# Gathering the query rows of destinations by indirect DMA in the fourth edge stage of a graph network kernel

## What is computed

```python
q = (tfn_features @ Wq).reshape(n, H, DQK)            # 8 heads of 16
x_dst = tfn_features[edge_dst]
wk = mlp2(edge_features, k_w1, k_b1, k_w2, k_b2)      # [E, 128]
wv = mlp2(edge_features, v_w1, v_b1, v_w2, v_b2)
k = tensor_product(x_dst, edge_sh, wk, Cqk)           # w * sum_s sh[:, s] * (x @ C[:, s, :]), s = 0..8
v = tensor_product(x_dst, edge_sh, wv, Cv)
attn = jnp.einsum('ehd,ehd->eh', q[edge_src], k)
# softmax over the edges of each node (segment max, exp, segment sum), then
upd = jax.ops.segment_sum(v * alpha[..., None], edge_src, num_segments=n) @ W_out
out = tfn_features @ W_self + upd                     # then batch norm, scale, shift
```

## Time and profile before

| | us |
|---|---|
| median of three runs | 3517.68 (3505.01 to 3533.71) |
| profiled execution | 3510.65 |
| its span, first to last instruction | 3508.9 |
| PE busy | 2551.3 (73%) |
| DVE busy | 2280.8 (65%) |
| POOL busy | 1789.0 (51%) |
| ACT busy | 1062.1 (30%) |

### The profile page before, as it was taken

One profiled execution on the slowest core, in us unless ns is written; L12 is line 12 of the kernel. 1 busy time (PEld: TensorE's weight loads), 2 busy tenths in 40 slices (PEclk: granted clock), 3 DMA queues, 4 the chain that ended last, 5 costly groups with the idle time before them and its releaser, 6 DMA issues. The chain is left out here.

```text
span 3508.9 us, 58176 instructions
## 1 busy us (share of the span) xinstructions
PE 2551.3 (73%) x14132; PEld 2166.8 (62%) x14132; DVE 2280.8 (65%) x5044; ACT 1062.1 (30%) x2723; POOL 1789.0 (51%) x1813
## 2 busy tenths in 40 slices
PE   3778777514554444357777765999999999999986
PEld 2778776413443333245555544888888888888872
DVE  3555555337887887855556542677777777777775
ACT  1111111134554564111111101344444344443441
POOL 2777776066666663157777723444444344443400
PEclk7776777556555666589999967999999999999985
DMA  2443443265554552035445517988888888888830
GB/s 64 93 87 84 87 87 64 46 161 131 132 123 125 132 124 72 2 110 157 153 153 161 158 63 177 203 204 197 197 201 199 200 198 190 193 200 198 195 92 9
DMA packets 433884, 475.50 MB, mean 136 GB/s; under 512 B 200837, under 2 KB 304648, under 8 KB 433712
## 3 DMA queue, kind: packets, MB, share of 16 engines
q1 hardware_dynamic: 358832, 295.60, 35.9%
q0 software_dynamic: 59904, 123.64, 15.2%
q10 hardware_dynamic: 14976, 54.53, 4.5%
HBM read 408.18 MB, written 65.34 MB: 135 GB/s over the span
## 5 line engine op out<-in xcount | busy, mean ns | idle before, releaser
L1960 PE MATMUL psum<-ckv,z 128*128 128x256 f32 x4160 | 969.7, 384 | 0.0
L1960 PEld LDWEIGHTS psum<-ckv,z 128*128 128x128 f32 x4160 | 767.9, 191 | 98.5
L1823 POOL DMA_INDIRECT ga<-XX,src_i x416 | 398.1, 957 | 449.7 <-PE psum L1941 307.0
L985 POOL DMA_INDIRECT ga<-T,src_i x416 | 431.4, 1037 | 302.3 <-issue 112.5
L275 POOL DMA_INDIRECT ga<-T,src_i x416 | 401.3, 965 | 151.7 <-issue 124.4
L275 POOL DMA_INDIRECT ga<-TA,src_i x416 | 412.4, 991 | 126.7 <-issue 126.7
L2009 DVE TENSOR_TENSOR z<-psum,shb 128x2560 f32<-128x2560 f32 x104 | 293.7, 2824 | 125.8 <-PE psum L1941 78.5
L455 PE MATMUL psum<-wre,re 128*128 128x68 f32 x832 | 213.4, 349 | 142.1 <-DVE oneT L331 82.6
L1816 POOL TENSOR_TENSOR acc<-acc,wkv 128x512 f32<-128x512 f32 x104 | 114.3, 1099 | 332.7 <-DMA wkv<-WKV 316.4
L455 PEld LDWEIGHTS psum<-wre,re 128*128 128x128 f32 x832 | 173.4, 258 | 162.9 <-issue 153.9
L2050 DVE TENSOR_TENSOR acc<-acc,psum 128x256 f32 x416 | 175.4, 422 | 120.2 <-PE psum L1932 90.9
(11 more groups left out here) (349 smaller groups left out, 4862.8 us busy)
## 6 DMA issues: line engine op xcount, KB each, us to landing
shb<-in_ea SPq DMA_DIRECT2D x104, 640.0 KB
WKV<-wkvo ACTq DMA_DIRECT2D x104, 512.0 KB
shb<-in_ea SPq DMA_DIRECT2D x104, 512.0 KB
wkv<-WKV SPq DMA_DIRECT2D x104, 512.0 KB
dl<-DL SPq DMA_DIRECT2D x312, 128.0 KB, 3.5
acc<-QW SPq DMA_DIRECT2D x416, 64.0 KB
win<-TB SPq DMA_DIRECT2D x416, 32.0 KB
ga<-T,src_i POOLq DMA_INDIRECT x832
```

Of the source, the lines that this page charges most:

```text
L985: pool.indirect_dma_start(ga[:, ring(g) + t, :], None, T1, bass.IndirectOffsetOnAxis(ap=src_i[:, g * GT + t:g * GT + t + 1], axis=0)).then ...
L1823: pool.indirect_dma_start(ga[:, (g % GR) * GT + t, :], None, XX, bass.IndirectOffsetOnAxis(ap=src_i[:, g * GT + t:g * GT + t + 1], axis=0) ...
L1960: last = pe.matmul(kv_of(k)[:, t, :], z[:, k % 2, j, t * 128:(t + 1) * 128], ckv[:, j, :], start=(j == 0), stop=(j == NZ - 1))
```

## The change

The query path by windows goes. Instead POOL gathers the query row of each edge's destination by indirect DMA, four a group, right behind the gather of features of the next group (`queries`), into a ring of four groups. DVE multiplies them with the weights at the head of `keys_and_values`. The loads of windows and places, ACT's three operations, PE's four matmuls and POOL's multiply are left out. The load of the weights loses its wait for POOL's multiply; it stays at two steps behind the harmonics. QW needs no padding rows any more, and the destinations of padding edges (-1) are raised to 0 by one DVE operation while the tables are made.

```diff
@@ tables of the fourth stage
-        QW = dram("QW", [NW, F])
+        QW = dram("QW", [N, F])
...
-                sp.dma_start(QW[N:NW, :], zero[:, 0:F]).then_inc(n3_o, 16)
...
                 ln_relu_steps(c, n3_var, n3_std, 1, XC=XC)
+                c.link(dve.tensor_scalar(dst_i[:], dst_i[:], 0, None, ALU.max))
                 dve.wait_ge(n3_p, 5)
...
+        QR = 4
+        e3_gq = [sem(f"e3_gq{k}") for k in range(UG)]
...
-        oneT = acc[:, 2, 0:2 * GT * W].rearrange("p (a e) -> p a e", a=2)
-        qs = acc[:, 2, 2 * GT * W:4 * GT * W].rearrange("p (a e) -> p a e", a=2)
-        win = acc[:, 2, 4 * GT * W:4 * GT * W + WR * GT * F].rearrange("p (t f) -> p t f", f=F)
+        qg = acc[:, 2, 0:QR * GT * F].rearrange("p (t f) -> p t f", f=F)
...
             def _(pool):
-                def weighted_query(g):
-                    slot = g % 2
-                    pool.wait_ge(e3_q, g + 1)
-                    pool.wait_ge(e3_n[slot], (g // 2 + 1) * 16)
-                    q = qs[:, slot, :].rearrange("p (t f) -> p t f", t=GT)
-                    pool.tensor_tensor(q, q, wkv[:, slot, :, 0:F], ALU.mult).then_inc(e3_wq, 1)
+                def queries(g):
+                    if g >= QR:
+                        pool.wait_ge(e3_ev, (g - QR + 1) * 2)
+                    for t in range(GT):
+                        pool.indirect_dma_start(qg[:, (g % QR) * GT + t, :], None, QW, bass.IndirectOffsetOnAxis(
+                            ap=dst_i[:, g * GT + t:g * GT + t + 1], axis=0)).then_inc(e3_gq[g % UG], 16)
...
-                    if g > GR:
-                        weighted_query(g - GR - 1)
-                for g in range(groups - GR - 1, groups):
-                    weighted_query(g)
+                    if g:
+                        queries(g - 1)
+                queries(groups - 1)
@@ SP
                 def weights_load(i, k):
                     g = i * UG + k
-                    wait(sp, e3_wq, g - 1)
-                    sp.sem_inc(e3_sp, 1)
                     wait(sp, e3_ev, (g - 1) * 2)
...
-                        wait(sp, e3_oT, g - 1)
-                        sp.sem_inc(e3_sp, 1)
-                        sp.dma_start(dl[:, k % 2, :], DL[:, cols].partition_broadcast(128)).then_inc(e3_dl[k % 2], 16)
...
-                        window_loads(win, sp, i, k, QW, F, e3_w, e3_Q, e3_sp, ring=WR)
@@ ACT: queries(i, k) and places(i, k) and their calls
-                    act.activation(qs[:, k % 2, :], bank[1][:], ACT.Copy).then_inc(e3_q, 1)
...
-                    act.activation(o, dl[:, k % 2, :], ACT.Abs, bias=iota_p[:, 0:1], scale=-1.0).then_inc(e3_ta, 1)
-                    act.wait_ge(e3_ta, g + 1)
-                    act.activation(o, o, ACT.Relu, bias=ones_c[:, 0:1], scale=-1.0).then_inc(e3_oT, 1)
@@ PE: queries(i, k) and its call
-                    for t in range(GT):
-                        last = pe.matmul(bank[1][:, t * 128:(t + 1) * 128], oneT[:, k % 2, t * 128:(t + 1) * 128],
-                                         win[:, (k % WR) * GT + t, :], start=True, stop=True)
@@ DVE
                 def keys_and_values(i, k):
                     g = i * UG + k
                     s, kk = k // KG, k % KG
+                    dve.wait_ge(e3_gq[k], i * 64 + 64)
+                    dve.wait_ge(e3_n[k % 2], i * (UG // 2 * 16) + (k // 2 + 1) * 16)
+                    q = qg[:, k % QR * GT:(k % QR + 1) * GT, :]
+                    dve.tensor_tensor(q, q, wkv[:, k % 2, :, 0:F], ALU.mult).then_inc(e3_wq, 1)
                     dve.wait_ge(e3_V, g + 1)
                     dve.wait_ge(e3_wq, g + 1)
                     wait(dve, e3_s, g)
                     three = lambda v: v.rearrange("p (t f) -> p t f", t=GT)
-                    dve.tensor_tensor(three(kt), kv_of(k)[:, :, 0:F], three(qs[:, k % 2, :]), ALU.mult).then_inc(e3_ev, 1)
-                    dve.wait_ge(e3_n[k % 2], i * (UG // 2 * 16) + (k // 2 + 1) * 16)
+                    dve.tensor_tensor(three(kt), kv_of(k)[:, :, 0:F], q, ALU.mult).then_inc(e3_ev, 1)
```

More of the change, by code:

```diff
@@ L1704, in _ @@
                 sp.wait_ge(n3_qc, len(rounds(NJ, 4)))
-                sp.dma_start(QW[0:N, :].rearrange("(j p) f -> p j f", p=PN), tab[:]).then_inc(n3_o, 16)
-                sp.wait_ge(n3_o, 4 * 16)
+                sp.dma_start(QW.rearrange("(j p) f -> p j f", p=PN), tab[:]).then_inc(n3_o, 16)
+                sp.wait_ge(n3_o, 3 * 16)
                 sp.wait_ge(n3_l, NL3 * 16)
@@ L1758, in build @@
         e3_g = [sem(f"e3_g{k}") for k in range(UG)]
-        WR = 2
-        e3_w = [sem(f"e3_w{k}") for k in range(WR)]
+        QR = 4
+        e3_gq = [sem(f"e3_gq{k}") for k in range(UG)]
         e3_e = [sem(f"e3_e{k}") for k in range(2)]
         e3_n = [sem(f"e3_n{k}") for k in range(2)]
[L1763 to L1766, removed]
+        (e3_one, e3_oa, e3_X, e3_z, e3_wq, e3_V, e3_ev, e3_s, e3_S, e3_acc, e3_M, e3_Mx, e3_i, e3_pad, e3_sp) = [
+            sem("e3_" + x) for x in
+            ("one", "oa", "X", "z", "wq", "V", "ev", "s", "S", "acc", "M", "Mx", "i", "pad", "sp")]
         S3 = softmax_sems("b3", bank[7])
@@ L1773, in build @@
         one = tmp("one3", [128, OR * GT, 128])
-        dl = tmp("dl3", [128, 2, GT * W], BF16)
         wkv = tmp("wkv", [128, 2, GT, 2 * F])
@@ L1900, in body @@
                     p1, p2 = soft_1(i, k), soft_2(i, k)
-                    if lag(i, k, 1):
-                        queries(*lag(i, k, 1))
                     if p1:
                         softmax_act_1(act, S3, p1[0] * 2 + p1[1], 8)
-                    if lag(i, k, 0):
-                        places(i, k)
                     if p2:
@@ L1942, in transposes @@
                     last.then_inc(e3_X, 1)
[L1944 to L1948, removed]
-                    for t in range(GT):
-                        last = pe.matmul(bank[1][:, t * 128:(t + 1) * 128], oneT[:, k % 2, t * 128:(t + 1) * 128],
-                                         win[:, (k % WR) * GT + t, :], start=True, stop=True)
-                    last.then_inc(e3_Q, 1)
                 def products(i, k, t):
@@ L1972, in body @@
                         transposes(i, k)
-                    if kv:
-                        queries(*kv)
                     if p1:
```

## The result

The changed kernel takes 3530.0 us (median; 3527.18 to 3534.63) against 3517.68 (3505.01 to 3533.71). The ratio is 1.004, with a 95% interval of 1.0021 to 1.0059: 0.4% slower, within the 1% of "no difference that can be told" and 6 us from the forecast. On another chip the same kernel was 8.8% slower than the kernel before (experiment 8). The profiled execution's span is 3525.4 us, 16.5 above that of before.

What follows compares the result with a forecast made beforehand. PE was taken as the bound by a small margin, DVE right behind. Terms 2 - 9 + 17 = +10 us gave 3520.7 on the profiled execution and 3527.7 for the median; the forecast between them was 3524 us, range 3488 to 3564.

Steps and rivals of the forecast that it cites:

- What bounds the kernel: Fourth edge stage: PE bound by a small margin, DVE right behind; PE's second sums wait for DVE's first addition.
- The price of the multiply: DVE, ahead of keys_and_values: the new multiply costs d = 0.80 us a step, bounds 0.69 and 1.10.
- dearer, 1.10 or more: Rival: DVE's new multiply costs 1.10 us or more a step, +29 us more, 3553 us; chance 0.20.
- The iteration: Eight steps of the stage's loop: 95.5 us against 95.3 before, DVE eating PE's 7.2; +2 us over 12 iterations.
- after k = 7 it starts 5.1: Loop's turn: DVE's z starts 5.1 us into PE's step k = 0, which then takes 14.8 us.
- The clock: TensorE's clock falls behind PE's standstill at k = 0: 2.3 us in 85% of twelve turns, less 6.8, +17 us.
- The first steps: First eight steps, without sums, PE alone: 5 us from the queries and 4 from POOL's multiply, -9 us in all.
- Queues and gathers: SP, POOL and DMA queues: the weights' load and the gathers stay hidden; eight gathers take 10.0 of some 11.9 us.
- The sum: Whole kernel: 2 - 9 + 17 = +10 us on the profiled execution's 3510.65 us, giving 3520.7 us.
- PE keeps its gain: Rival: the 94 us of queries' work taken off PE come through whole, 3420 us; chance 0.10.

Runs made afterwards that it cites:

- experiment 8: Another chip, kernel before 3868.68 us: changed kernel 4204.18 us (1.0879); with a second DVE multiply 4211.23 us; late multiply, unlooped DVE and extra PE matmuls 4172.99 us.
- Experiment 1: Changed kernel with four unused matmuls put back on PE in each step, where the queries' matmuls stood: 3553.81 us, ratio 1.0126 to the kernel before.
- experiment 2: Changed kernel with DVE's new multiply done one step earlier, behind the addition of the first sums: 3491.39 us, ratio 0.9955 to the kernel before.
- experiment 3: Changed kernel with sixteen unused matmuls on PE at k = 0, ahead of its second sums: 3510.35 us, ratio 1.0002 to the kernel before.
- experiment 4: Changed kernel without query gathers from the ninth group on, old rows multiplied again: 3529.45 us, ratio 1.0054 to the kernel before.
- experiments 6 and 7: 6: DVE's stage program unlooped: before 3464.37, changed 3444.75, changed with late multiply 3406.08 us. 7: the last plus four unused PE matmuls per step: 3461.88 us.

## Why the prediction came out

**What bounds the kernel: right.** PE the bound by a small margin, DVE right behind it, and the second sums the place where they meet. Experiment 1 shows it from one side (0.9 us more on PE change nothing in k = 2, 3, 4), experiment 2 from the other.

**The price of the multiply: right.** d = 0.80 was taken; the rows give 0.77 in a plain step and 0.88 at the turn (2422.84 - 2421.96), and L1976 itself is 0.686, L2033 was 0.687. The rival "dearer, 1.10 or more" fell with it. The Trainium skill's rule (SBUF — State Buffer, Who interferes with whom) that a GpSimd instruction reading SBUF blocks DVE's with two SBUF inputs holds for POOL's tensor_tensor (before, every L598 of over 430 ns overlaps L1816; without it the median went from 835 to 429 ns) but not for gathers: 57 of the 104 multiplies overlap one, and the longest took 704 ns.

**The iteration: right in its steps, short at the turn.** By step, in us:

| k | before | predicted | after |
|---|---|---|---|
| 1, 5 | 11.30 | 10.39 | 10.40 |
| 2, 6 | 11.87 | 11.94 | 12.11, 12.01 |
| 3, 7 | 11.87 | 12.33 | 12.36 |
| 4 | 11.30 | 11.39 | 11.38 |
| 0, without the clock's fall | 13.93 | 14.8 | 15.6 |
| sum | 95.3 | 95.5 | 96.6 |

The 13.93 is one turn (the eleven of before take 14.15 on average without the falls); the 15.6 is the mean of eleven (18.1) less 2.45; experiment 3, with the clock held, shows 15.44 to 15.83. Of the 1.1 us, k = 2 and 6 have 0.24 and the turn 0.8. In k = 2 DVE allowed the second sums 0.05 us later than worked out, and PE's part behind them took 3.18 instead of 3.06: where PE has stood, its first pair of second sums takes 0.49 us instead of 0.39. At the turn the step "after k = 7 it starts 5.1" is the one that was off: z came 5.6 to 6.3 us behind PE, because the issue pause was 3.6 to 4.3 us and not the 3.33 of the earlier trace rows (3.0 to 3.4 in all turns before), and DVE waited 0.65 us for the exponents ahead of L1994, where it was 0.30 before (L2033). Why the pause grew is not shown. Without the clock this term is +12 over ten iterations, where it was +2 over twelve.

**The clock: right in kind, a little short in size.** Taken were 2.3 us in 85% of twelve turns. It fell in all eleven turns of the loop, behind standstills of 4.7 to 5.5 us, and cost 2.2 to 2.8 us each time, 26.9 in all, less 6.8: +20 instead of +17. The twelfth "turn" is the entry into the loop, where PE stood only 1.06 us in the changed kernel; the prediction had counted it, and the 4.57 us of before there were POOL's doing. Experiment 3 confirms the clock as a cost of its own: with it held, k = 0 is 2.4 us shorter. The price does not follow the standstill alone: in experiment 1 PE stood 3.8 to 4.2 us at each turn, and the part behind took 4.5 to 4.6 us in five turns and 5.7 in six. The Trainium skill (TensorE: Matmul & The Clock Gate, Part 1: The HAM clock gate) has the array fall to half rate after idle stretches; the windows agree (PEclk 0.99, then 0.50, behind a stretch with PE at 0.00).

**The first steps: near.** -9 predicted for the first eight with POOL's lead; the first sixteen gave -12.3 (80.5 + 99.93 to 75.31 + 92.85 us), 2.3 of it the clock's. The first eight alone gave -5.2; 4.4 more lie in the entry into the loop, where DVE no longer waits for POOL's multiply.

**Queues and gathers: right.** Hidden, by experiment 4.

**The sum.** Predicted -9 + 2 + 17 = +10. Measured in the spans: -10 in the first sixteen steps without the clock, +12 in the ten iterations without it, +20 for the clock, together +22.3 in the stage; -5.8 around it, +16.5; in the medians +12.3. The iteration's term was too small by 10 us and the clock's by 3. The 6 us ahead of the stage, which nobody predicted, hid a part, and they are scatter. That the forecast was closer than its terms is luck.

**The rival "PE keeps its gain"** is false for this kernel and true for a neighbour: with the multiply late and the turn gone, the same change is worth 58 us and PE is the bound again (experiments 6 and 7), for the wait that gave its gain away is nearly gone.

## What to carry to other kernels

Work taken off the busiest engine is worth only the slack of the engine that it waits for: before moving an operation onto that one, write down for each step of the unrolled body when it releases the other, and count the operation only where it lies ahead of that release. Then place it behind the release; here the order alone was worth 0.85%, more than the change. A loop's turn is paid by the engine that has no slack left there, and the other's standstill is paid twice when its clock falls.

## What the runs showed of the hardware

- A turn of DVE's loop costs 3.0 to 3.4 us of "issue" before z in the kernel before and 3.6 to 4.3 in the changed one; written out, there is none, and the kernel before alone gains 1.4% (48 us, against 3512.05 on the same chip).
- TensorE's granted clock went to 0.50 at all eleven turns where PE had stood 4.7 to 5.5 us. Before, it fell behind standstills of 2.09, 2.95 and 4.57 us and held behind nine of 2.25 to 2.89. A fall cost 1.6 to 2.8 us in the matmuls behind it, and sixteen idle matmuls in the gap prevented it.
- Indirect gathers on POOL (0.95 us each, twice as many as before) left DVE's multiply of 128x512 alone (at most 704 ns); a POOL tensor_tensor of 128x512 stretched DVE's scan L598 from 428 to up to 1272 ns.
- Two chips of the same kind took 3518 and 3869 us for the kernel before, and 3530 and 4204 for the changed one: on the second a load that is hidden on the first ends the wait for z, and the change costs 8.8% instead of 0.4%. A verdict of this size holds for the chip that it was measured on.
